# Attention stage of a cross-attention and soft-MoE kernel: a new instruction order and a new map of PSUM banks

## The reference

```
x = x + attention(layernorm(x), ctx)          # 32 heads of 8, axial rope on q and k, softmax over 64 keys
    q = layernorm(x) @ Wq ; k, v = split(ctx @ Wkv)
    w = softmax(rope(q) . rope(k) / sqrt(8)) ; attention = (w @ v) @ Wout + bout
x = x + ffn(layernorm(x))                      # soft mixture of 16 experts with 128 slots each
```

## Time and profile before

| | |
|---|---|
| time, median of 3 runs | 519.87 us (518.77 to 519.9) |
| the profiled execution | 519.52 us, of which the span (first to last instruction) 517.6 us |
| busy share of the span | PE 92%, DVE 68%, ACT 59%, POOL 28% |
| attention stage, to the first product of the ffn stage | about 212 us of the span |
| mean granted clock of TensorE | 0.970 of full speed |

### The profile page before, as it was taken

One profiled execution on the slowest core, in us unless ns is written; L12 is line 12 of the kernel. 1 busy time (PEld: TensorE's weight loads), 2 busy tenths in 40 slices (PEclk: granted clock), 3 DMA queues, 4 the chain that ended last, 5 costly groups with the idle time before them and its releaser, 6 DMA issues.

```text
span 517.6 us, 13978 instructions
## 1 busy us (share of the span) xinstructions
PE 476.5 (92%) x5296; PEld 389.6 (75%) x5296; DVE 351.6 (68%) x858; ACT 305.7 (59%) x611; POOL 146.0 (28%) x247
## 2 busy tenths in 40 slices
PE   0668999998999999999999999999999999999995
PEld 0536677776666675988888888888888888888884
DVE  5687888888788896475575657657565765756562
ACT  1346566566665655526745854774585477458543
POOL 3509611139794721211311121121112112111100
PEclk9969999999999996699999999999999999999998
DMA  6600000027003000000000000000000000000000
GB/s 172 245 7 6 7 6 8 7 85 173 11 5 65 5 1 1 1 3 1 13 12 4 10 10 10 0 10 10 0 10 10 10 0 10 10 0 10 11 12 11
DMA packets 16016, 12.72 MB, mean 25 GB/s; under 512 B 7232, under 2 KB 15344, under 8 KB 15600
## 3 DMA queue, kind: packets, MB, share of 16 engines
q1 hardware_dynamic: 15984, 12.27, 8.3%
HBM read 10.16 MB, written 2.11 MB: 24 GB/s over the span
## 4 chain that ended last, share of the span: by engine, by line
PE 70%; DVE 14%; ACT 8%; issue 4%; SPq 1%; DMA 1%; DVEq 0%; POOL 0%; ACTq 0%
PE psum L951 14%; PE psum L952 13%; PE psum L953 13%; PE psum L1163 8%; PE psum L1178 7%; PE psum L1016 4%; PE psum L1001 4%; DVE mx L696 3%; PE psum L1033 3%; ACT vb L493 3%; DVE pb L701 3%; PE psum L1051 2%; DVE pb L865 2%; DVE xT_l L665 2%; ACT mu_raw L563 2%
## 5 line engine op out<-in xcount | busy, mean ns | idle before, releaser
L563 ACT COPY mu_raw<-psum 128x384 f32<-128x384 f32 x96 | 41.0, 445 | 104.4 <-PE psum L1163 104.4
L843 DVE TENSOR_REDUCE es<-eb 128x4 f32<-128x512 f32 x64 | 43.1, 686 | 64.9 <-ACT eb L555 64.9
L1163 PE MATMUL psum<-w_raw,eb 64*128 64x129 f32 x1024 | 66.6, 279 | 1.1 <-DVE pb L865 0.2
L1163 PEld LDWEIGHTS psum<-w_raw,eb 64*128 64x128 f32 x1024 | 60.4, 187 | 6.4 <-DVE pb L865 4.2
L483 ACT COPY pT<-psum 128x512 f32<-128x512 f32 x64 | 36.7, 601 | 41.5 <-PE psum L1016 41.5
L350 POOL TENSOR_TENSOR sm<-sm,mhalf 128x1 f32<-128x1 f32 x16 | 8.8, 550 | 174.2 <-DVE sm L822 174.2
L696 DVE TENSOR_REDUCE mx<-psum 128x8 f32<-128x512 f32 x64 | 41.1, 684 | 21.8 <-PE psum L1001 21.8
L1016 PEld LDWEIGHTS psum<-ident,pb 128*128 128x128 f32 x256 | 29.5, 150 | 34.0 <-issue 27.0
L1016 PE MATMUL psum<-ident,pb 128*128 128x128 f32 x256 | 44.5, 302 | 11.0 <-ACT vb L493 8.9
L479 ACT ACTIVATE pb<-pb 128x512 f32<-128x512 f32 x64 | 38.2, 629 | 27.2 <-DVE pb L701 27.2
L951 PE MATMUL psum<-mun_h,xlT_l 128*128 128x512 f32 x128 | 53.2, 415 | 0.0
(11 more groups left out here) (156 smaller groups left out, 1071.1 us busy)
## 6 DMA issues: line engine op xcount, KB each, us to landing
mu_raw<-in_L_ffn_mu SPq DMA_DIRECT2D x1, 2048.0 KB, 13.1
out<-w_raw SPq DMA_DIRECT2D x16, 128.0 KB, 1.7
xa<-in_x SPq DMA_DIRECT2D x1, 1536.0 KB, 8.7
ctile<-in_ctx SPq DMA_DIRECT2D x16, 64.0 KB, 1.9
eb<-mur_scratch SPq DMA_DIRECT2D x1, 1024.0 KB, 5.0
w_raw<-in_L_ffn_W SPq DMA_DIRECT2D x2, 512.0 KB, 8.0
w_raw<-in_L_ffn_W SPq DMA_DIRECT2D x1, 1024.0 KB, 7.9
xa<-in_x SPq DMA_DIRECT2D x1, 512.0 KB, 3.6
```

The costliest lines, as they stand in the source:

```text
L563: a.copy(eT[:, e0:e0 + n, :].rearrange("p n (b k) -> p b n k", b=2), pair(i, n)[:, :, :, HC:XC]).then_inc(eT_ready, 1)
L1163: m = mm(bank[HB[i % 3] + b][:, n * XC:(n + 1) * XC], eb[rows, e, :], xw[rows, e, :], start=True, stop=True)
```

## The change

- PE's `logits(t)` makes all sixteen matmuls of a tile in one run, at the head of the step, over four row groups and two column halves. It waits once for q, both parts of k, and for the whole softmax of the tile before.
- The order of PE's step becomes: logits, transposes of the probabilities of groups 0 and 1, `project_qk`, (`mu_sums`), `transpose_o`, transposes of groups 2 and 3, `project_out`, `transpose_kq`, `transpose_x`, `attend`, `project_v`.
- `transpose_kq` writes bank 4, over q and k ahead of rope, and no longer waits for `sub_done`; one semaphore step instead of two. `attend` writes bank 5 and waits for the residual of s-2 instead of the rope of s+1. The sums of `mu_sums` move to the last 16 columns of bank 5, and PE waits for `muss_clamped` in step 6 instead of step 7.
- ACT: `pT_copy` 0 and 1, `exp_group` 0 and 1, `oT_copy`, `pT_copy` 2 and 3, `q_copy`, `k1_copy`, `xT_high`, `exp_group` 2 and 3, `v_copy`.
- DVE: `residual` (and the clamp of the sums) moves ahead of `softmax(s, p, 2)`; `k0_copy` reads bank 4 and waits for `k1_copy` too.
- `xT` has two buffers, so `project_v` can run behind `transpose_x`.

```diff
-            def logits(t, g0, half):
-                if half:
-                    pe.wait_ge(k1_ready, t * 4 + 4)
-                else:
-                    pe.wait_ge(q_ready, t + 1)
-                    pe.wait_ge(k0_ready, t + 1)
-                for b in range(2):
-                    for g in (g0, g0 + 1):
+            def logits(t):
+                pe.wait_ge(q_ready, t + 1)
+                pe.wait_ge(k1_ready, t * 4 + 4)
+                pe.wait_ge(k0_ready, t + 1)
+                wait(pe, sub_done, t * 4)
+                for half in range(2):
+                    for b in range(2):
+                        for g in range(GROUPS):
...
             def transpose_kq(t):
                 pe.wait_ge(qk_roped, t * 2 + 2)
-                wait(pe, sub_done, t * 4)
-                nc.tensor.transpose(bank[2][:, 0:P], qkr[:, 1, 0:P], ident[:]).then_inc(kq_filled, 1)
...
             def attend(t, p, bo=5):
-                if roped:
-                    pe.wait_ge(qk_roped, t * 2 + 6)
+                if bo == 5:
+                    wait(pe, x1_ready, t)
...
             def step(s, p, ...):          # PE
+                logits(s)
                 if before:
-                    transpose_p(s - 1, 1 - p, 0, more=after)
-                logits(s, 0, 0)
-                if before:
-                    transpose_p(s - 1, 1 - p, 1, more=after)
-                logits(s, 0, 1)
-                if before:
-                    transpose_p(s - 1, 1 - p, 2)
+                    for gr in range(2):
+                        transpose_p(s - 1, 1 - p, gr, more=after)
+                if after and before:
+                    project_qk(s + 1, 1 - p)
                 if norms is not None:
                     mu_sums(s, norms)
                 if out:
-                    transpose_o(s - 2, clamped)
-                if after and before:
-                    project_qk(s + 1)
-                logits(s, 2, 0)
+                    transpose_o(s - 2)
                 if before:
-                    transpose_p(s - 1, 1 - p, 3)
-                logits(s, 2, 1)
+                    for gr in range(2, GROUPS):
+                        transpose_p(s - 1, 1 - p, gr)
                 if out:
                     for k in range(KD):
                         project_out(s - 2, k)
                 if after:
-                    project_v(s + 1)
-                    if before:
-                        attend(s - 1, 1 - p)
                     transpose_kq(s + 1)
                     if ahead:
                         transpose_x(s + 2, p)
+                if norms == 3:
+                    pe.wait_ge(muss_clamped, 1)
+                if before:
+                    attend(s - 1, 1 - p, 5 if after else 4)
+                if after:
+                    project_v(s + 1, 1 - p)
...
             def k0_copy(t, b=4):          # DVE
+                dve.wait_ge(kq_filled, t + 1)
+                if b == 4:
+                    dve.wait_ge(k1_ready, t * 4 + 4)
...
             def step(s, p, ...):          # ACT
                 if before:
-                    for gr in range(3):
+                    for gr in range(2):
                         pT_copy(s - 1, gr)
-                    if out:
-                        oT_copy(s - 2)
-                    pT_copy(s - 1, 3)
-                for gr in range(GROUPS):
+                for gr in range(2):
+                    exp_group(s, p, gr)
+                if out:
+                    oT_copy(s - 2)
+                if before:
+                    for gr in range(2, GROUPS):
+                        pT_copy(s - 1, gr)
+                if after:
+                    q_copy(s + 1)
+                    k1_copy(s + 1)
+                    if ahead:
+                        xT_high(s + 2, p)
+                for gr in range(2, GROUPS):
                     exp_group(s, p, gr)
                 if after:
                     v_copy(s + 1, 1 - p)
-                    q_copy(s + 1)
-                    if ahead:
-                        xT_high(s + 2)
-                    k1_copy(s + 1)
```

More of the change, by code:

```diff
@@ L525, in step @@
                     v_copy(s + 1, 1 - p)
-                    q_copy(s + 1)
-                    if ahead:
-                        xT_high(s + 2)
-                    k1_copy(s + 1)
             act.wait_ge(consts_dve, 3)
-            xT_high(0)
+            xT_high(0, 0)
             v_copy(0, 0)
-            xT_high(1)
+            xT_high(1, 1)
             act.wait_ge(hmask_step, 2)
-            q_copy(0)
-            k1_copy(0)
-            step(0, 0, before=False)
+            q_copy(0, 3)
+            k1_copy(0, 3)
+            step(0, 0, before=False, out=False)
             step(1, 1, out=False)
@@ L677, in rope_sums @@
             def rope_sums(t):
-                wait(dve, kq_filled, t * 2)
+                wait(dve, kq_filled, t)
                 dve.wait_ge(ropeab_done, t * 2 + 2)
@@ L747, in step @@
                 if ahead:
-                    xT_low(s + 2)
+                    xT_low(s + 2, p)
             dve.wait_ge(wqkv_step, 1)
@@ L752, in _ @@
                 .then_inc(wqkv_ready, 1)
-            xT_low(0)
+            xT_low(0, 0)
             dve.wait_ge(sin_ready, 1)
@@ L763, in _ @@
             rope_products(0)
-            xT_low(1)
+            xT_low(1, 1)
             rope_sums(0)
@@ L771, in _ @@
             dve.wait_ge(hmask_step, 2)
-            k0_copy(0)
+            k0_copy(0, 2)
             dve.wait_ge(x_loaded[1], 16)
@@ L789, in _ @@
             k0_copy(1)
-            xT_low(2)
+            xT_low(2, 0)
             with dve.Fori(AHEAD // 4 + 1, TILES // 4) as i:
@@ L912, in _ @@
             xlT_copy(0)
-            normalise(TILES - 2)
+            normalise(TILES - 2, 4)
             dve.wait_ge(wb_loaded, 96)
@@ L924, in _ @@
             slot_sums(0, range(2, 4))
-            normalise(TILES - 1)
+            normalise(TILES - 1, 4)
             dve.wait_ge(xw_const, 3)
@@ L963, in transpose_x, with project_qk @@
                 nc.tensor.transpose(bank[7][:, 2 * P:3 * P], ctile[:, p, :], ident[:]).then_inc(xT_filled, 1)
-            def project_qk(t):
+            def project_qk(t, p):
                 pe.wait_ge(xT_ready, t + 1)
-                wait(pe, on_ready, t - 2)
                 for k in range(KD):
-                    mm3(bank[4][:, 0:DIM], [h[:, k, :] for h in xT], [h[:, k, :] for h in wqkv],
+                    mm3(bank[4][:, 0:DIM], [h[:, p, k, :] for h in xT], [h[:, k, :] for h in wqkv],
@@ L978, in project_v, with transpose_kq @@
                     .then_inc(v_filled, 1)
[L980 removed]
+            def transpose_kq(t, b=4, b0=4):
                 pe.wait_ge(qk_roped, t * 2 + 2)
[L983 to L987 removed]
@@ L989, in logits @@
[L989 to L1004 removed]
+                for k in range(KD):
+                    nc.tensor.transpose(bank[b][:, k * P:(k + 1) * P], qkr[:, 0, k * P:(k + 1) * P], ident[:])
@@ L1097, in step @@
                         transpose_x(s + 2, p)
+                if norms == 3:
[4 more added lines that the diff above has]
+                    project_v(s + 1, 1 - p)
             transpose_x(0, 0)
             pe.wait_ge(wqkv_ready, 1)
-            project_qk(0)
-            project_v(0)
+            project_qk(0, 0)
+            project_v(0, 0)
             transpose_x(1, 1)
-            transpose_kq(0)
-            project_qk(1)
+            transpose_kq(0, 3, 2)
+            project_qk(1, 1)
             step(0, 0, before=False, out=False)
@@ L1111, in _ @@
                 step(3 + q, (3 + q) % 2, norms=q)
-            step(7, 1, clamped=True)
+            step(7, 1)
             with pe.Fori(4, TILES // 2 - 1) as i:
@@ L1203, in _ @@
             step(TILES - 1, 1, after=False, ahead=False)
-            attend(TILES - 2, 0, roped=False)
             pe.wait_ge(sub_done, TILES * 4)
@@ L1217, in _ @@
             slot_logits(0, range(3, 4))
-            attend(TILES - 1, 1, roped=False)
+            attend(TILES - 1, 1, 4)
             pe.wait_ge(w12_ready, 2)
```

69 lines of the change are left out of this document (34 added, 35 removed).

## The result

The changed kernel takes 499.59 us (median of 4 executions, 497.97 to 500.33), the kernel before 519.32 (4 executions beside it): the ratio is 0.969 (0.961 to 0.976), so it is 3.1% faster. The prediction was 501 in 494.5 to 511. The profile of before (519.52 us, clock 0.970) is of the second group and holds the 16.9 us at the lower level of the earlier trace rows. Twice the difference in clock between the groups (0.983 less 0.967), times its span of 517.6 us, is 16.6 us at the lower level, about that one stretch.

A forecast was written before the change was run, and what follows sets the result against it. PE led with DVE close behind; DVE would become the bound. Steps, two late inputs, 2.2 us of corrections and a 3.5 us clock fall gave ffn start 194.8 against 212.43, 17.6 off 519.52: 501.9, given as 501, range 494.5 to 511.

The forecast's parts named there:

- What bounds the kernel now: Attention steps: PE leads, DVE a close second; PE shorter by over about 1.5 us a step leaves DVE the bound.
- What the change takes from PE: PE's attention step: one run of sixteen logits and two of eight transposes save 1.75 us, to about 8.6.
- The new step, by the clock: Attention step timed from DVE's first maximum: 9.78 us, DVE's work of 9.5 plus the residual's wait of 0.27.
- the correction of 0.17: Added to every attention step, as the same table gave 11.13 us for the old step where the trace has 11.31.
- Two late inputs: xn of tile 4 makes step 2 cost 12.0 us; context tile 10 makes step 8 cost 11.4.
- The sum: Attention stage to the first ffn product: 191.3 us with step corrections, 194.8 with a clock fall, against 212.43 before.
- D of step 1: Start of DVE's first maximum in step 1: forecast at 36.8 us, where it was 38.74.
- The 3.5 us for a fall at the end of the stage: Cost of PE's clock falling again some 3 us ahead of the last transposes of step 14.
- (a): The forecast itself: DVE the bound in the attention steps, 498 to 505 us; chance 0.55.
- (b): Clock holds through the attention stage's end, or a late input does not bind: 494 to 498 us; chance 0.17.
- (c): Loop through k0_copy, logits and maximum outlasts DVE's work: up to 511.5 us; smaller misses 505 to 509; chance 0.16.
- (d): PE's clock falls inside the loop, 4.4 us per stretch; one to four stretches 0.07, more 0.05.

The follow-up runs named there:

- the filler: One unread 256-column product in PE's idle time ahead of each step's logits, added to the kernel with both late inputs mended: 493.06 us, 0.957 of the kernel before.
- the kernel with four calls: The changed kernel with the logits again in four calls of four matmuls between PE's other work: 540.00 us, 1.040 of the kernel before.

## Why the prediction was right, and where it was not

**What bounds the kernel now.** The result of this step, that PE's step shrinks by more than 1.5 us and leaves DVE the bound, was right: one more maximum costs its full length, one more product of PE nothing, and without the residual's wait DVE works with no gap. The reading under it was half right. I took DVE's wait of 1.35 us for room and the step for PE's work plus small waits. The kernel before with 0.60 us more on DVE lost 0.6 a step and kept the wait: the step was a loop, and DVE's work up to the second subtraction was part of it. The table of the step had the loop in it; the sentence drawn from the waits did not.

**What the change takes from PE.** Right within 0.07: the run of sixteen was put at 1.13 us to the next start and 1.12 to the first maximum, and took 1.06 (142.88 to 143.94) and 1.17 (142.88 to 144.05). The eight transposes take 1.04 to 1.09, and 0.84 to the next start (144.78) where 0.9 was taken. A matmul of wo, which uses all 128 rows and the same 256 columns, took 0.43 us of PE as the filler (two records), so sixteen one by one would be some 6.9 us by this estimate: the run is about six times faster. The Trainium skill, "TensorE: Matmul & The Clock Gate", section "Part 3: Packing small matmuls — row/col tiling", gives 3.07 times for four row groups with 512 columns. The run here is another packing, eight tiles with 256 columns, and the trace neither confirms nor contradicts that figure.

**The new step, by the clock.** 9.78 us by the table, 9.95 with the correction of 0.17. Measured: 9.77 once (101.83 to 111.60) and 9.98 in the one undisturbed step behind 120 us (144.05 to 154.03), and 9.98 to 10.01 in the steps of the kernel with the context tile early from 112 to 162 us, with the residual waiting 0.26 where 0.27 was forecast, behind project_out behind oT_copy, as named. Moving oT_copy ahead of one exp takes the step to 9.62, and the residual then starts 4.39 us behind the first maximum instead of 4.74: the whole difference lies at this wait, so it was the only one on the bound. k0_copy's wait for k1_copy cost nothing. Steps 3 to 6 were put at 41.6 and took 41.53. The first maxima of those steps do wait 0.23 to 0.24 us for the logits, slightly over the 0.2 that was named. With the table's 9.5 of DVE work the step ought to have been bound by PE's side as closely as by DVE's; DVE's work is in fact 9.62, and PE had room for the 0.43 us of the filler with 0.34 left.

**Two late inputs.** Both where they were expected. Context tile 10: step 8 was put at 11.4 and took 11.37. xn of tile 4: PE's wait was put at 2.8 and was 2.55, but step 2 took 14.94 instead of 12.0. The term that was missed is the clock behind that wait: 6.7 us at the lower level. I had counted the wait and not a fall behind it. In the other profile of the changed kernel the fall came a step earlier and the wait not at all; steps 1 and 2 then took 21.9 us together instead of 24.2 (21.4 forecast).

**The sum.** D of step 1 was 36.15 for 36.8; steps 9 to 12 took 41.96 for 39.8 with the correction, because of two short falls; step 13, 11.14 for 11.2; the end of the stage, 8.0 for 8.1. Without any clock term the sum was 191.3; measured was 193.99. The 3.5 us for a fall at the end of the stage did not come. Its reason, that the waits which the clock fell behind are still there, was no rule: the clock held there in this profile, as it held there in the kernel before with one more maximum, and as it seems to hold in the executions of before near 512.4 us. The forecast took its start from the one profile with that fall, so some 6 us of the 212.43 it started from were a fall that the kernel before does not always have. Instead 2.9 us went to the fall behind the xn wait and some 2 to the two falls in the loop. So the total is right within 0.8 us of the trace because a term of 3.5 at the wrong place stood for one of about 5 at others, less 2.4 us of surpluses elsewhere (0.65 at D of step 1, and most of the corrections of 0.17 in steps 1 to 8). The figure of 501 is better than its reasons: the mechanism held, the clock's term was the right size by luck. The forecast's own sum, besides, gives 501.9, which rounds to 502; no term stands behind the step to 501.

**The rivals.** (a) came, at 499.6. Of (b), the clock did hold at the end. (c) did not: no loop longer than DVE's work. (d) did come in its small form: one fall of 6.7 and two of 3.3 us where the forecast had a chance of 0.12 for any and expected a granted clock of 1.00 from 41 to beyond 175 us. It was priced right in kind, 4.4 us for 10.2 us at the lower level, as PE has no room of that size. That it can decide the sign is shown by a relative of the changed kernel, the one with the residual late: its undisturbed step, 11.06 us, is shorter than the 11.31 of before, yet with a granted clock of 0.90 from 60 to 120 us it takes 524 us. The forecast held against (d) that the idle share of a step is hardly larger than before; it did not look at the single waits. Between 41 and 196 us the longest wait of PE before is 0.73 us, and the one of 1.05 comes at 196.83, 1 us ahead of the fall. But the length of a wait does not settle it either. In the profile shown here the falls start behind waits of 2.55, 0.73 and 0.78 us, while steps 3 to 5 pass with 1.05 to 1.07 and no fall. What makes a fall in a given step is open: the same kernel had them at 54, 132 and 163 us in one profile and at 43, 118, 142 and 173 in another.

## What to carry to other kernels

A wait that stands in each step with the same length is not room until one adds work ahead of it and sees the wait shrink; a fixed piece of 0.6 us on the waiting engine is a cheap probe. The probe only tells where the added work stands: put it where no chain to the wait begins, or remove the wait and see whether the engine then works without a gap. When a schedule is shortened until two engines are nearly even, price falls of TensorE's clock as well: in the kernel with the residual late, five of the seven waits of 1.83 us had 3.4 or 6.8 us at half clock behind them. Such a fall can also swallow a later wait, so that removing that wait gives nothing in the median. Look at the granted clock of several executions of the kernel before, and not of one profile, before its time is taken as the start of a forecast: here that choice was worth 6 of 20 us. A new order and a new buffer map that belong together can each lose alone (4% and 8% here) and gain some 3% as one; test them together before judging either.

## What the runs showed of the hardware

In the loop of the changed kernel and its relatives the clock of TensorE fell behind single waits from 0.43 us (with oT_copy moved, at 117 us) to 2.71 us (both inputs early, at 43 us). It stayed at the lower level for 3.3 to 13.7 us though PE hardly stood in it (busy 13.29 of 13.50 us in the longest, at 88 to 102 us of the kernel with four calls). In the steps of before, 11.31 us with single waits of 0.64 to 0.73 us, nothing fell in 157 us. With only the context tile early PE had waits of up to 1.17 us and no fall from 61 to 484 us. The same kernel's clock fell at other places in another execution.

Sixteen matmuls of 32 rows by 64 columns and 256 moving columns take 1.12 us at 2.4 GHz (2.01 at 1.2 GHz), and 1.18 to 1.29 with another order, so matmuls on different tiles overlap over several instructions, not only between neighbours. One fp32 matmul over the full height, with the same 256 columns, takes 0.43 us of PE.
